# Attention in a decoder kernel: the denominators of 128 queries of a group move from TensorE to ScalarE

## The chip, the cores and the metric

The kernel runs on one core of one Trainium2 chip. The metric is the device time of one execution in microseconds (us), from the first to the last instruction and the little that lies around them; the median of several runs is quoted. Every number of one execution comes from its profile.

## What is computed

A decoder layer over 4 sequences of 512 tokens with 512 channels: attention and layer norm, then a layer in which each token goes to one of four experts, then a layer with eight routed experts and a shared one. The change lies in the attention, whose core is this:

```
qkv = x @ w_attn + b_attn
q, k, v = split(qkv)                       # 16 heads of 32 channels
att = einsum('bhqd,bhkd->bhqk', q, k) / sqrt(32)
att = where(causal, att, -inf)
att = softmax(att, axis=-1)
y = einsum('bhqk,bhkd->bhqd', att, v)
x = layernorm(x + (y @ w_proj + b_proj))
```

A softmax needs for each query and head the maximum of its scores and, as the denominator, the sum of their exponentials.

## The kernel before, in words

The attention works on **groups** of 4 heads (128 channels), 4 groups per sequence, 16 groups in all (g = 0 to 15). A sequence is cut into 4 tiles of 128 tokens. One list of steps, written out by `attention_steps`, sets the order on every engine; each engine walks the same list and does its own part of each entry. The entries that matter:

- **Q, K**: a product of 512x512 results made in three parts of four matmuls each (high times high, low times high, high times low). ScalarE writes the rounded half `ch_hi` (L624), VectorE the remainder `ch_lo` (L771). Then both are copied within SBUF to the stacked operands `qS` and `kS`, 24 transfers of 64 KB for one group: SyncE issues 20 of them (L362), ScalarE the other four, `kS` from `ch_hi` (L629), right behind K's L624. Q of the next group waits on ScalarE (L623) until all 24 have landed, since it overwrites `ch_hi`.
- **P1** (g, 0 to 9), "first scores": queries on partitions. TensorE writes one 512-column bank of `psS` (L548), VectorE adds the mask and takes the maximum (L787) into `rowmax`. `psS` has two banks, so unit n waits for the maximum of unit n-2 (L545). Units 0 to 3 hold the last 128 queries (tile 3) of one head against all 512 keys, as one block; units 4 to 7 hold a block of 384 and one of 128; units 8 and 9 two of 256.
- **M**: the maxima are transposed into four rows (L556) and ScalarE writes them, negated, as four more rows of `qS` (L647).
- **P2** (g, 0 to 9), "second scores": keys on partitions, maxima already subtracted. TensorE writes a bank of `psE` (L569), ScalarE takes the exponential into `p_f` (L657), GpSimd clears what lies above the diagonal (L424). `psE` has two banks, so unit n waits for the exponential of unit n-2 (L566).
- **PV** (g, j), in the order j = 0, 1, 3, 2: TensorE multiplies the exponentials with the values into `psO` and with ones into `psN`, which gives the denominators (L587), over (4-j)*128 query columns.
- **NORM** and **YH**: VectorE turns and inverts the denominators and scales `psO` in three parts (L794 to L804); ScalarE and GpSimd split the result (L664, L429).
- PR is the projection with `w_proj`, V the product for the values, XT and CW are transposes of inputs and of weights of the next layer, ZB adds a bias (L438, GpSimd), LN1 and LN2 are the layer norm.

**Step s** (0 to 15) overlaps three groups: Q and K of group s+2, P1 of group s+1, P2 of group s, PV of group s-1. It begins with a **head**: six product parts of Q and K, with the first three P1 units and M between them. Then PV with P1 and P2 between, then pairs of P1 and P2. Where nothing else is to be filled in, the last three P2 units (7, 8, 9) are left over and stand in the next head, one behind each part of Q. I call such steps **short**: s = 2, 3, 6, 7, 10, 11 (and step 1 is close to them). Steps 4, 8, 12 are filled with V and steps 5, 9, 13 with PR, twelve product parts each: the **long** steps. Steps 14 and 15 have no Q and K left.

Before step 0 stand Q and K of groups 0 and 1 and P1 of group 0. There ScalarE issues all 12 transfers of each K itself (L636, L640).

## Time and profile before

| | us |
|---|---|
| median of 3 runs | 1248.32 |
| lowest, highest | 1247.42, 1250.17 |
| the profiled execution | 1241.62 |
| its span, first to last instruction | 1239.9 |
| TensorE busy in the span | 1177.1 (95%) |
| VectorE, ScalarE, GpSimd busy | 683.6, 452.9, 280.7 |

The attention fills about the first 410 us of the span. Busy time of TensorE is modelled for matmuls that overlap one another, so a busy TensorE may still have been slowed by what feeds it. The trace has a view in order of time for each engine, with the wait before an instruction and what ended it in square brackets; a view by stretches; a view by groups of instructions; and the chain, which follows the work that ended last back in time.

### The profile page before, as it was taken

How to read it: one execution, taken by the hardware profiler on the slowest of the kernel's cores; microseconds unless marked ns; L12 is line 12 of the kernel's file. 1: busy time of each engine (PE TensorE's matmuls, PEld its weight loads, DVE VectorE, ACT ScalarE, POOL GpSimd, SP SyncE). 2: the span in 40 equal slices, each digit the busy share in tenths (PEclk: the TensorE clock that was granted, in tenths of full speed). 3: DMA queues.
4: the chain of work that ended last, by engine and by line, in shares of the span. 5: the costliest groups of instructions: out<-in, count | busy, mean ns of one | idle time of the engine just before them, and what ended most of it. 6: DMA issues, size and time to landing. Idle time of an engine off the chain costs nothing.

```text
span 1239.9 us, 20255 instructions
## 1 busy us (share of the span) xinstructions
PE 1177.1 (95%) x6404; PEld 930.3 (75%) x6404; DVE 683.6 (55%) x1485; ACT 452.9 (37%) x699; POOL 280.7 (23%) x405
## 2 busy tenths in 40 slices
PE   7789999999998789998999999999999998999995
PEld 6556676676675478886677888999999997778884
DVE  5575666656656547765467434434335433766744
ACT  3245434434436223322333334334434433323331
POOL 3012314414415301223122430000000001452302
PEclk8989999999999989999999999999999999999998
DMA  7347673423433233333166673344444523555530
GB/s 249 79 117 246 201 265 105 135 68 86 137 85 123 90 111 95 112 117 119 31 98 138 236 272 104 108 150 156 145 148 150 161 86 100 189 187 165 160 118 34
DMA packets 128814, 169.76 MB, mean 137 GB/s; under 512 B 18112, under 2 KB 71360, under 8 KB 128704
## 3 DMA queue, kind: packets, MB, share of 16 engines
q1 hardware_dynamic: 110368, 128.77, 34.7%
q0 software_dynamic: 10336, 32.53, 7.3%
q10 hardware_dynamic: 8000, 7.10, 2.4%
q8 instruction: 56, 0.92, 0.3%
q14 instruction: 54, 0.44, 0.1%
HBM read 95.98 MB, written 47.19 MB: 115 GB/s over the span
## 4 chain that ended last, share of the span: by engine, by line
PE 79%; DVE 7%; DMA 6%; ACTq 2%; ACT 2%; issue 2%; POOL 2%; SPq 1%; POOLq 0%; DVEq 0%
PE bank L852 28%; PE bank L913 15%; PE psT L482 12%; PE psS L548 3%; DMA shared_raw<-in_L_ffn_Sd_dram 3%; PE psO L587 3%; PE bank L1533 3%; PE bank L1534 3%; PE bank L1535 3%; PE psE L569 2%; PE psN L587 2%; PE bank L1555 1%; DVE psS L787 1%; PE bank L1578 1%; SPq L362 1%
## 5 line engine op out<-in xcount | busy, mean ns | idle before, releaser
L913 PE MATMUL bank<-store,shared_held 128*128 128x512 f32 x792 | 188.0, 393 | 3.6 <-issue 2.9
L913 PEld LDWEIGHTS bank<-store,shared_held 128*128 128x128 f32 x792 | 149.0, 189 | 38.5 <-DVE shared_held L1852 4.3
L482 PE MATMUL psT<-store 128*128 128x512 f32 x576 | 157.6, 409 | 4.3 <-DVE store L701 2.7
L657 ACT ACTIVATE acc<-psE 128x512 f32<-128x512 f32 x160 | 92.8, 598 | 133.0 <-PE psE L569 89.3
L787 DVE CUSTOM_DVE_ANT_0 psS<-psS,attn_mask 128x512 f32<-128x512 f32 (+3 forms) x256 | 120.0, 514 | 35.5 <-PE psS L548 35.2
L482 PEld LDWEIGHTS psT<-store 128*128 128x128 f32 x576 | 106.2, 196 | 24.0 <-issue 3.0
L1447 POOL DMA_INDIRECT routed_rows_io<-sorted_y,routed_pos x32 | 37.1, 1159 | 376.6 <-DMA sorted_y<-routed_rows_io 313.0
L852 PE MATMUL bank<-shared_held,routed_h_hi 128*128 x624 | 115.9, 328 | 0.3 <-DVE routed_h_lo L1893 0.3
L424 POOL TENSOR_SCALAR_AFFINE_SELECT acc<-acc 128x256 f32<-128x256 f32 (+1 forms) x160 | 56.9, 362 | 258.4 <-ACT acc L657 258.0
L852 PEld LDWEIGHTS bank<-shared_held,routed_h_hi 128*128 128x128 f32 x624 | 100.3, 188 | 0.7 <-issue 0.5
L852 PE MATMUL bank<-store 128*128 x351 | 91.5, 405 | 0.0
L548 PE MATMUL psS<-attn_kS,attn_qS 96*128 96x512 f32 (+3 forms) x256 | 73.9, 352 | 8.8 <-DVE attn_rowmax L787 4.4
L548 PEld LDWEIGHTS psS<-attn_kS,attn_qS 96*128 96x128 f32 x256 | 44.8, 196 | 48.2 <-DVE attn_rowmax L787 20.7
L569 PE MATMUL psE<-attn_qS,attn_kS 100*128 100x512 f32 (+3 forms) x256 | 69.9, 338 | 4.9 <-ACT acc L657 4.2
L852 PEld LDWEIGHTS bank<-store 128*128 128x128 f32 x351 | 63.6, 190 | 12.2
L1654 ACT ACTIVATE routed_h_f<-bank 128x512 f32<-128x512 f32 x44 | 26.3, 597 | 123.5 <-PE bank L913 123.5
L1533 PE MATMUL bank<-shared_held,routed_h_hi 128*128 128x512 f32 x176 | 69.8, 397 | 0.1
L1534 PE MATMUL bank<-shared_held,routed_h_hi 128*128 128x512 f32 x176 | 69.5, 395 | 0.0
L1535 PE MATMUL bank<-shared_held,routed_h_lo 128*128 128x512 f32 x176 | 69.2, 393 | 0.0
L913 PE MATMUL bank<-shared_held 128*128 128x512 f32 x264 | 65.0, 400 | 0.8 <-DVE shared_held L1852 0.7
L1852 DVE TENSOR_TENSOR shared_held<-shared_raw,shared_held 128x1024 fp32r<-128x1024 f32 x42 | 51.3, 1221 | 24.4 <-ACT shared_held L1641 24.2
L852 PE MATMUL bank<-shared_held,routed_h_lo 128*128 x312 | 62.7, 323 | 0.0
(273 smaller groups left out, 1995.7 us busy)
## 6 DMA issues: line engine op xcount, KB each, us to landing
sorted_x<-attn_zero SPq DMA_DIRECT2D x19, 768.0 KB, 6.3
shared_raw<-in_L_ffn_Sg_dram SPq DMA_DIRECT2D x44, 256.0 KB, 3.1
shared_raw<-in_L_ffn_Su_dram SPq DMA_DIRECT2D x44, 256.0 KB, 3.6
shared_raw<-in_L_ffn_Sd_dram SPq DMA_DIRECT2D x44, 256.0 KB, 4.8
routed_rows_io<-sorted_x SPq DMA_DIRECT2D x39, 256.0 KB, 2.9
sorted_y<-routed_rows_io SPq DMA_DIRECT2D x39, 256.0 KB, 2.1
attn_qS<-attn_ch_hi SPq DMA_DIRECT2D x128, 64.0 KB
routed_gu_raw<-in_L_ffn_Wg_dram SPq DMA_DIRECT2D x8, 704.0 KB, 4.5
```

The costliest lines, as they stand in the source:

```text
L424: pool.affine_select(out=at, in_=at, compare_op=ALU.is_ge, fill=drop, base=0, pattern=[[0, at.shape[1]], [1, P]], channel_multiplier=-1).t ...
L482: last = pe.matmul(out, lhs[a](k), rhs[c](k), start=(s[-1] == 0 and k == 0), stop=(s[-1] == 2 and k == KC - 1))
L548: last = pe.matmul(psS[:, n % 2, c0:c0 + (t + 1) * P], q[0:AUX, i, t * P:(t + 1) * P], k[0:AUX, i, 0:(t + 1) * P], start=True, stop=True)
L569: last = pe.matmul(psE[:, n % 2, c0:c0 + (QT - j) * P], k[0:AUX + 4, i, j * P:(j + 1) * P], q[0:AUX + 4, i, j * P:T], start=True, stop=True)
L587: last = pe.matmul(to[i * D:(i + 1) * D, j * P:T], values(i), p_f[:, u, c0:c0 + (QT - j) * P], start=(j == 0), stop=(j == 2), tile_positio ...
L657: act.activation(p_f[:, u, :], psE[:, n % 2, :], ACT.Exp, scale=SCALE).then_inc(exp_done, 1)
L787: last = dve.tensor_tensor_reduce(scores, scores, mask[:, (3 - t) * P:T], 1.0, BELOW_ALL, ALU.add, ALU.max, rowmax[:, g % 2, t, i:i + 1])
L852: last = pe.matmul(out, lhs[a](k), rhs[c](k), start=(n == 0), stop=(n == 3 * chunks - 1))
L913: last = pe.matmul(out, w[:, slot, at + k * P:at + (k + 1) * P], x_part(k), start=(g == 0 and k == 0), stop=(g == 2 and k == KC - 1))
L1533: pe.matmul(s_y[i], h[0], w[0], start=(c == 0), stop=False)
L1534: pe.matmul(s_y[i], h[0], w[1], start=False, stop=False)
L1535: last = pe.matmul(s_y[i], h[1], w[0], start=False, stop=(c == CH - 1))
```

## The change

Three things change in the attention, and some semaphores are merged (the constants and one-hot rows now count on one semaphore, the same instructions in the same order).

1. The denominators of tile 3, the last 128 queries, are no longer made by TensorE. ScalarE takes the exponential of the first scores in `psS` in place, with the maximum as bias, and totals each row (64 instructions, four in each group). So that both exponentials use the same maximum, VectorE rounds it (`rounded`) and scales it (`shift`), two instructions of one column behind each of those units. GpSimd spreads the totals over 128 columns, and TensorE transposes them into the last 128 columns of `psN`. The matmuls with ones shrink by 128 columns, and those of j = 3 go.
2. The P1 units come in another order of blocks, so that the four totalled ones stand at positions 3, 5, 7 and 9. The unit two behind waits for the total, no longer for the maximum.
3. ScalarE's four key transfers for group s+2 move from K in the head to behind the exponential of P2 unit 5.

```diff
+    BLOCKS = (8, 9, 4, 0, 5, 1, 6, 2, 7, 3)
     def s_segments(u):
+        u = BLOCKS[u]
...
@@ GpSimd
+                elif kind == "M":
+                    g = s[1]
+                    pool.wait_ge(total_done, 4 * (g + 1))
+                    if g >= 2:
+                        pool.wait_ge(pv_done, QT * (g - 2) + 1)
+                    pool.tensor_copy(spread_3[:, g % 2, :].rearrange("p (i d) -> p i d", d=D),
+                                     total_3[:, g % 2, :].unsqueeze(2).broadcast_to([P, 4, D])).then_inc(spread_done, 1)
...
@@ TensorE, P1
                     if n >= 2:
-                        pe.wait_ge(max_done, n - 1)
+                        of, was = divmod(n - 2, UNITS)
+                        if summed_block(was) is not None:
+                            pe.wait_ge(total_done, 4 * of + summed_block(was) + 1)
+                        else:
+                            pe.wait_ge(max_done, n - 1)
...
@@ TensorE, PV
-                    for to, values in ((psO, lambda i: v_f[...]), (psN, lambda i: ones[:])):
-                        for i in range(4):
+                    if j == 0:
+                        pe.wait_ge(spread_done, g + 1)
+                        pe.transpose(psN[:, T - P:T], spread_3[:, g % 2, :], ident[:])
+                    for to, values, upto in ((psO, lambda i: v_f[...], T),
+                                             (psN, lambda i: ones[:], T - P)):
+                        for i in range(4 if j * P < upto else 0):
...
@@ ScalarE
+            def totals(upto):
+                for n in range(summed[0], upto):
+                    g, u = divmod(n, 4)
+                    scores = psS[:, (g * UNITS + BLOCKS.index(u)) % 2, :]
+                    act.wait_ge(shift_done, 2 * n + 2)
...
+                    act.activation(scores, scores, ACT.Exp, bias=shift[:, g % 2, u:u + 1], scale=SCALE,
+                                   accum_out=total_3[:, g % 2, u:u + 1]).then_inc(total_done, 1)
+                summed[0] = max(summed[0], upto)
...
@@ ScalarE, Q and K
-                    if qk == 1 and g >= 2:
-                        act.wait_ge(hi_done, hi_order[s[:2]] + 1)
-                        for i in range(4):
-                            act.dma_start(kS[g % 3][2 * D:3 * D, i, :].bitcast(F32), ...
...
+                elif kind == "P1":
+                    g, u = s[1:]
+                    if g == 0:
+                        totals(seen[0])
+                    if summed_block(u) is not None:
+                        seen[0] = 4 * g + summed_block(u) + 1
                 elif kind == "M":
+                    totals(seen[0])
...
@@ ScalarE, P2
+                    totals(ripe[0])
+                    ripe[0] = seen[0]
                     act.wait_ge(e_full, n + 1)
...
                     act.activation(p_f[:, u, :], psE[:, n % 2, :], ACT.Exp, scale=SCALE).then_inc(exp_done, 1)
+                    if u == 5 and g + 2 < NG:
+                        g += 2
+                        act.wait_ge(hi_done, hi_order["K", g] + 1)
+                        for i in range(4):
+                            act.dma_start(kS[g % 3][2 * D:3 * D, i, :].bitcast(F32), ...
...
@@ VectorE, P1
+                    u = summed_block(u)
+                    if u is not None:
+                        dve.wait_ge(max_done, n + 1)
+                        dve.tensor_copy(rounded[:, g % 2, u:u + 1], rowmax[:, g % 2, QT - 1, u:u + 1]).then_inc(shift_done, 1)
+                        dve.wait_ge(shift_done, 8 * g + 2 * u + 1)
+                        dve.tensor_scalar(shift[:, g % 2, u:u + 1], rounded[:, g % 2, u:u + 1].bitcast(F32), -SCALE, None,
+                                          ALU.mult).then_inc(shift_done, 1)
```

Where it moves instructions shows in the order on the engines. First ScalarE in a short step, from K's rounded half to the end of the next Q; `acc<-psE` is the exponential of P2, `attn_qS<-psT` belongs to M, `attn_yT_hi` to YH. Before:

```order
L647 ACTIVATE attn_qS<-psT 4x2048
L624 ACTIVATE attn_ch_hi<-psT,attn_bqk 128x512
L629 DMA attn_kS<-attn_ch_hi 32x512 x4
L657 ACTIVATE acc<-psE 128x512 x7
L664 CAST attn_yT_hi<-acc 128x512
L657 ACTIVATE acc<-psE 128x512 x2
L624 ACTIVATE attn_ch_hi<-psT,attn_bqk 128x512
```

Now, in the same place, with line numbers of the changed kernel (L629 is a total, L701 the exponential, L706 the key transfers), from the second exponential on:

```order
L629 ACTIVATE psS,attn_total<-psS,attn_shift 128x512
L701 ACTIVATE acc<-psE 128x512 x2
L629 ACTIVATE psS,attn_total<-psS,attn_shift 128x512
L701 ACTIVATE acc<-psE 128x512 x2
L629 ACTIVATE psS,attn_total<-psS,attn_shift 128x512
L701 ACTIVATE acc<-psE 128x512
L706 DMA attn_kS<-attn_ch_hi 32x512 x4
L701 ACTIVATE acc<-psE 128x512
L714 CAST attn_yT_hi<-acc 128x512
L629 ACTIVATE psS,attn_total<-psS,attn_shift 128x512
L701 ACTIVATE acc<-psE 128x512 x2
L664 ACTIVATE attn_ch_hi<-psT,attn_bqk 128x512
```

The transfers stood ahead of the exponential of unit 0 and now stand between those of units 5 and 6; a total stands ahead of those of units 1, 3, 5 and 7, the last behind YH.

Second, ScalarE before step 0, from Q of group 1 to Q of group 2. Before:

```order
L624 ACTIVATE attn_ch_hi<-psT,attn_bqk 128x512 x2
L636 DMA attn_kS<-attn_ch_hi 32x512 x8
L640 DMA attn_kS<-attn_ch_lo 32x512 x4
L624 ACTIVATE attn_ch_hi<-psT,attn_bqk 128x512
L647 ACTIVATE attn_qS<-psT 4x2048
```

Now (L671 and L675 are the transfers of K of group 1):

```order
L664 ACTIVATE attn_ch_hi<-psT,attn_bqk 128x512
L629 ACTIVATE psS,attn_total<-psS,attn_shift 128x512 x2
L664 ACTIVATE attn_ch_hi<-psT,attn_bqk 128x512
L671 DMA attn_kS<-attn_ch_hi 32x512 x8
L675 DMA attn_kS<-attn_ch_lo 32x512 x4
L629 ACTIVATE psS,attn_total<-psS,attn_shift 128x512
L664 ACTIVATE attn_ch_hi<-psT,attn_bqk 128x512
L629 ACTIVATE psS,attn_total<-psS,attn_shift 128x512
```

Two totals of group 0 stand ahead of the twelve transfers; the third, for which P1 unit 9 of group 0 waits, behind them.

Third, TensorE in the PV part of a step. Before:

```order
L587 MATMUL psO<-acc 32x512 x4
L587 MATMUL psN<-acc,attn_ones 32x512 x4
L548 MATMUL psS<-attn_kS,attn_qS 128x512
L569 MATMUL psE<-attn_qS,attn_kS 128x512
L587 MATMUL psO<-acc 32x384 x4
L587 MATMUL psN<-acc,attn_ones 32x384 x4
```

Now (L609 is the transpose of the totals, L614 PV, L569 P1, L592 P2):

```order
L609 MATMUL psN<-ident,attn_spread 128x128
L614 MATMUL psO<-acc 32x512 x4
L614 MATMUL psN<-acc,attn_ones 32x384 x4
L569 MATMUL psS<-attn_kS,attn_qS 128x512
L592 MATMUL psE<-attn_qS,attn_kS 128x512
L614 MATMUL psO<-acc 32x384 x4
L614 MATMUL psN<-acc,attn_ones 32x256 x4
```

One transpose came in and every matmul with ones lost 128 columns; P1 and P2 stand where they stood.

## Rows read from the trace of the kernel before

**Rows 1.** Busy time by stretch: stretch, its length, then each engine, granted clock, DMA

```profile
200.00:300.00 100.00, 98.31 (x654) 67.01 (x645) 63.03 (x198) 42.76 (x66) 33.43 (x63) 1.00 0.37 101
```

**Rows 2.** The chain through step 11: start, us on the chain, what

```profile
306.04 0.60 PE psT L556 x4
...
307.79 0.99 PE psO L587 x8
308.79 0.86 PE psN L587 x8
...
311.09 0.65 PE psN L587 x8
...
312.81 0.22 PE psN L587 x8
...
314.32 0.43 PE psN L587 x8
...
325.51 0.99 PE psO L587 x8
```

**Rows 3.** ScalarE in order of time, step 11 and the next head: start, us, instruction [wait]

```profile
309.28 2.67 ACTq L629 DMA_DIRECT2D attn_kS<-attn_ch_hi  x4
...
316.94 0.60 ACT L657 ACTIVATE acc<-psE 128x512 f32<-128x512 f32 x1 [0.28 <-PE psE L569]
...
317.69 0.60 ACT L657 ACTIVATE acc<-psE 128x512 f32<-128x512 f32 x1 [0.15 <-PE psE L569]
...
319.80 0.62 ACT L664 CAST attn_yT_hi<-acc 128x512 fp32r<-128x512 f32 x1 [1.51 <-DVE acc L804]
...
320.33 1.08 ACT L657 ACTIVATE acc<-psE 128x512 f32<-128x512 f32 x2
```

**Rows 4.** TensorE in the same stretch: P1 unit 7, P2 units 6, 8 and 9

```profile
315.33 0.41 PE L548 MATMUL psS<-attn_kS,attn_qS 96*128 96x384 f32 x2
...
317.26 0.40 PE L569 MATMUL psE<-attn_qS,attn_kS 100*128 100x384 f32 x2
...
319.67 0.41 PE L569 MATMUL psE<-attn_qS,attn_kS 100*128 100x256 f32 x2
...
320.97 0.50 PE L569 MATMUL psE<-attn_qS,attn_kS 100*128 100x256 f32 x2
```

**Rows 5.** VectorE in order of time: two small instructions in a row, and one maximum

```profile
284.08 0.17 DVE L832 BATCH_NORM_AGGREGATE attn_mv<-attn_stats 128x2 f32<-128x6 f32 x1
284.28 0.15 DVE L834 TENSOR_SCALAR attn_veps<-attn_mv 128x1 f32<-128x1 f32 x1
...
306.51 0.73 DVE L787 CUSTOM_DVE_ANT_0 psS<-psS,attn_mask 128x512 f32<-128x512 f32 x1
```

**Rows 6.** ScalarE's groups by line: count, busy us, mean ns, idle before

```profile
L624 ACT ACTIVATE attn_ch_hi<-psT,attn_bqk 128x512 fp32r<-128x512 f32 x32 | 22.0, 688 | 38.8 <-PE psT L482 26.4 <-DMA attn_kS<-attn_ch_lo 12.0
```

**Rows 7.** SyncE's last four key transfers of step 11, and P1 unit 0 behind them

```profile
316.12 2.50 SPq L362 DMA_DIRECT2D attn_kS<-attn_ch_lo  x4
...
322.19 0.19 PEld L548 LDWEIGHTS psS<-attn_kS,attn_qS 96*128 96x128 f32 x1 [0.22 <-DMA attn_kS<-attn_ch_lo]
```

**Rows 8.** ScalarE and TensorE in order of time, before and in step 0

```profile
46.76 0.50 PE L548 MATMUL psS<-attn_kS,attn_qS 96*128 96x256 f32 x2
...
50.26 2.53 ACTq L640 DMA_DIRECT2D attn_kS<-attn_ch_lo  x4
...
54.28 0.50 PE L548 MATMUL psS<-attn_kS,attn_qS 96*128 96x512 f32 x1 [2.44 <-DMA attn_kS<-attn_ch_lo]
...
59.09 2.67 ACTq L629 DMA_DIRECT2D attn_kS<-attn_ch_hi  x4
...
65.08 0.79 PE L569 MATMUL psE<-attn_qS,attn_kS 100*128 100x512 f32 x1 [2.75 <-ACT acc L657]
```

**Rows 9.** TensorE in the PV part of step 4: P2 unit 2

```profile
141.95 0.51 PE L569 MATMUL psE<-attn_qS,attn_kS 100*128 100x512 f32 x1 [0.71 <-ACT acc L657]
```

More of the change, by code:

```diff
@@ L164, in key_of, with summed_block @@
         return s[:-1] if s[0] in PARTS else s
+    BLOCKS = (8, 9, 4, 0, 5, 1, 6, 2, 7, 3)
+    def summed_block(u):
+        return BLOCKS[u] if BLOCKS[u] < 4 else None
     def s_segments(u):
+        u = BLOCKS[u]
         if u < 4:
@@ L216, in attention_phase @@
         rowmax = sb("rowmax", [P, 2, QT, 4], F32)
+        rounded = sb("rounded", [P, 2, 4], F32R)
+        shift = sb("shift", [P, 2, 4], F32)
+        total_3 = sb("total_3", [P, 2, 4], F32)
+        spread_3 = sb("spread_3", [P, 2, P], F32)
         rsum = sb("rsum", [P, T // D], F32)
@@ L280, in attention_phase @@
         max_done = sem("max_done")
+        shift_done = sem("shift_done")
+        total_done = sem("total_done")
+        spread_done = sem("spread_done")
         e_full = sem("e_full")
@@ L554, in _ @@
                     pe.wait_ge(max_done, UNITS * (g + 1))
+                    pe.wait_ge(shift_done, 8 * (g + 1))
                     for t in range(QT):
-                        last = pe.transpose(out[0:4, t * P:(t + 1) * P], rowmax[:, g % 2, t, :], ident[:])
+                        maxima = rowmax[:, g % 2, t, :] if t < QT - 1 else rounded[:, g % 2, :].bitcast(F32)
+                        last = pe.transpose(out[0:4, t * P:(t + 1) * P], maxima, ident[:])
                     give(s, last)
@@ L583, in _ @@
                                 pe.wait_ge(sh_free[bank_of["V", g // 4, i]], use_of["V", g // 4, i] + 1)
-                    for to, values in ((psO, lambda i: v_f[:, j, (g % 4) * P + i * D:(g % 4) * P + (i + 1) * D]), (psN, lambda i: ones[:])):
-                        for i in range(4):
+                    if j == 0:
+                        pe.wait_ge(spread_done, g + 1)
+                        pe.transpose(psN[:, T - P:T], spread_3[:, g % 2, :], ident[:])
+                    for to, values, upto in ((psO, lambda i: v_f[:, j, (g % 4) * P + i * D:(g % 4) * P + (i + 1) * D], T),
+                                             (psN, lambda i: ones[:], T - P)):
+                        for i in range(4 if j * P < upto else 0):
                             u, c0 = E_AT[j, i]
-                            last = pe.matmul(to[i * D:(i + 1) * D, j * P:T], values(i), p_f[:, u, c0:c0 + (QT - j) * P],
+                            last = pe.matmul(to[i * D:(i + 1) * D, j * P:upto], values(i), p_f[:, u, c0:c0 + upto - j * P],
                                              start=(j == 0), stop=(j == 2), tile_position=(0, i * D))
@@ L762, in _ @@
                     then(dve.tensor_reduce(picked1, picked, AX, ALU.add))
-                    dve.tensor_copy(place[:], picked1).then_inc(place_done, 1)
-                    dve.wait_ge(place_done, 1)
+                    then(dve.tensor_copy(place[:], picked1))
                 elif kind in ("Q", "K") and s[-1] == 2:
```

34 lines of the change are left out of this document (17 added, 17 removed).

## The prediction

> **What bounds the kernel now.** Read the view by stretches first: inside the attention TensorE is busy 98% of the time at full clock, VectorE 63, ScalarE 43 [rows 1]. That invites the sum "less work for TensorE, less time". The chain through step 11 says how far it holds: of the step's 17.7 us (325.51 less 307.79) nearly all lies on TensorE, the denominators among it with 0.86, 0.65, 0.22 and 0.43 [rows 2]. Then read the other queues for how near they are. ScalarE and TensorE in order of time show that P2 units 8 and 9 come 2.4 and 3.7 us behind unit 6, and the exponentials they wait for just in time [rows 3, 4]. SyncE's twenty transfers are as near: the last is issued by 318.62, and P1 unit 0 of the next group waits 0.22 us for its landing at 322.19 [rows 7]. So in short steps three resources are level. The long steps have twelve product parts between the P1 and P2 units, and there only TensorE counts.
>
> **What TensorE saves.** The matmuls with ones run over 512, 384, 256 and 128 columns, 1280 in all, in 0.86 + 0.65 + 0.43 + 0.22 = 2.16 us [rows 2], 1.69 us for a thousand columns. The change leaves 768: 0.86 us less. It adds one transpose of 128 columns; four in M take 0.60 [rows 2], so between 0.15 and, with a weight load that nothing hides, 0.3; 0.2 taken. Net 0.65 us a group, 10.4 for 16 groups, if nothing else moves.
>
> **What the others get.** VectorE: two small instructions behind each of 64 maxima. Two such in a row stand 0.20 us apart [rows 5]: 0.4 a unit, 26 us in all, hidden at 63% busy except where someone waits for that unit. ScalarE: 64 exponentials of 128x512 with a column as bias. An exponential without one takes 0.60 [rows 3], a pass with one 0.69 [rows 6]; the total of a row, which no row shows, may add something like nothing or another 0.14. 0.69 taken, the ends 0.60 and 0.83. 44 us in all, again hidden except on a chain. GpSimd: 16 copies of 128x128, early enough for PV a step later: nothing. The block order itself: the same columns, nothing. The merged semaphores: nothing.
>
> **The new chain.** P1 unit 9 waits for the total of unit 7: matmul 0.4, maximum 0.73 [rows 5], two small ones 0.4, total 0.69, hand-offs 0.1: 2.3 us. Before it was 0.4 + 0.73. And the exponential of unit 5 stands behind that total on ScalarE.
>
> **A short step, walked through in the clock of step 11.** Before, P1 unit 7 starts at 315.33, P2 unit 6 at 317.26, unit 8 at 319.67, unit 9 at 320.97 [rows 4]. After:
> - The four PV parts ahead save 0.65; the total of unit 5 takes some 0.15 back. P1 unit 7 at 314.8.
> - Its total is ready 2.3 later, 317.1, so P1 unit 9 starts at 317.15 and P2 unit 6 at 317.45. The saving is already gone, 0.2 late.
> - ScalarE: the exponential of unit 5 until 317.7, then the four key transfers. In the head they take 2.67 [rows 3] and delay the first exponential, but PV lies there and TensorE doesn't wait. Here they end at 320.4, and the exponential of unit 6, which before followed at 317.69 [rows 3], ends at 321.0. P2 unit 8 at 321.1: 1.4 late.
> - Queued behind: YH 0.62 [rows 3], the total of unit 9 0.69, the exponential of unit 7 0.60, ends 322.95. P2 unit 9 at 323.0: 2.0 late.
> - Two waits go: the 0.22 of P1 unit 0 [rows 7] and about as much ahead of M. Left: 1.6 at the end of the step; over six short steps, two of which have more idle time there, **1.5 each, +9.0**.
>
> The figure that weighs most is 0.67 us for one issue on ScalarE. The Trainium skill ("DMA: Bandwidth & Descriptors", Anatomy of one DMA — SWDGE (gpsimd) path) gives about 50 ns for a sequencer's dispatch, of which the data's travel is no part. By it four issues hold ScalarE 0.2 us, a short step loses some 0.3 instead of 1.5, and the kernel would come out near 1250.5. The trace has 2.67 for four on this very queue, and the trace decides.
>
> **The start.** Totals of group 0 stand in ScalarE's order at the P1 steps. That of unit 7, for which P1 unit 9 waits, comes behind K of group 1 and its twelve transfers, the last issued by 52.79 [rows 8]. So unit 9 starts at 53.5 and not at 46.76. TensorE had 2.44 us of waiting ahead of P1 unit 0 of group 1 [rows 8], which cover a part: +4.3. In step 0 the four transfers (2.67 at 59.09) leave the way of the first exponential, for which P2 unit 2 waited 2.75 at 65.08 [rows 8]: -2.7. But no PV lies between the P1 units there, and units 5, 7 and 9 each wait for a total: 2.3 in place of two maxima, 1.5: three times 0.8, less what is hidden, +1.9. Together **+3.5** (bounds +1 and +6: the first if the twelve issues turn out hidden by the wait on landing, the second if nothing is hidden).
>
> **The rest.** Step 1, nearly a short one, with two transposes between that cover the wait for the total: +1.2. Six long steps: at least four filled slots lie between the exponentials of unit 5 and unit 8, some 5 us, which hide transfers and totals: 0.65 gained each, -3.9. In step 4 the wait of 0.71 behind slow transfers [rows 9] goes: -0.7. Step 14 is paced by VectorE (maxima, layer norm, splits), where the small instructions come on top: 4 x 0.4 less 0.65, +1.0. In step 15 GpSimd's wait for its input hides all: 0. The last PV: -0.65.
>
> **Sum**: 9.0 + 1.2 + 3.5 - 3.9 - 0.7 + 1.0 - 0.65 = +9.4 us. On the profiled execution's 1241.6 that is 1251.0; the median of the runs is 6.7 above it, so 1248.3 + 9.4 = **1257.7 us**.
>
> **The rivals.**
> - **TensorE's saving comes through.** If the exponential of unit 6 is not late, since the issues are shorter there or the step has slack that rows 4 don't show, each group keeps its 0.65: 10.4, and 0.7 and 2.7 for the transfers that leave the head, less 4.3 at the start: -9.5, **1238.8**. For it: 98% busy [rows 1], the chain on TensorE [rows 2]. Against it: the order of unit 6 behind the transfers. The Trainium skill ("Perfetto Trace Analysis", Identifying the Most-Contended Engine) tells to optimize the engine with the highest occupancy first; here that is TensorE, and by it this rival would win.
> - **The two cancel.** Short steps lose 0.3 and not 1.5, the start and the rest as above: 9.4 - 7.2 = +2.2, about 1250; a cheaper start brings it to 1247. It decides by how long ScalarE is held between the exponentials of units 5 and 6: below about 1.4 us P2 unit 8 no longer waits.
> - **The key transfers land too late.** Issued by 320.4 and landing 3.6 us behind the issue, as SyncE's do (318.62 to 322.19, rows 7), they come at 324.0, just when P1 unit 0, now at 323.8, wants them; and Q's rounded half waits for all 24. It bites from a landing of over 3.6 us on. With 2 us more in each short step: +12 on top, **1269**. For it: zero-filling transfers are in flight in steps 1 to 5 and an input load in steps 7 and 11.
>
> **How the numbers follow.** The forecast, a loss of 4 to 16 us, gets 0.58; the saving coming through 0.20; cancelling 0.10; late transfers 0.12. The range: the forecast's case runs from 1252 to 1264 by the ends of the total's price (0.6 to 0.83, twice in a short step: 2 to 3 us) and of the start. It reaches down into the first rival, to 1240, and up to most of the last, 1268; outside lie about 0.1 below and 0.05 above. About 0.2%, 2.5 us, is what a measurement of this kernel can tell from no change. Faster by more: 0.21, the first rival and a sliver of the second. Within: 0.10. Slower by more: 0.69.
>
> **What would show it.** In the profile after: TensorE busy some 7 to 10 us less, the span longer; P2 units 8 and 9 of short steps waiting on the exponential for 1 us and more; the transfers in one piece of 2.6 us on ScalarE between two exponentials; short steps of 19.2 us and long ones shorter by 0.65; P1 unit 9 of group 0 near 53.5. It would be wrong if P2 unit 8 doesn't wait, if the totals take well over 0.83, or if P1 unit 0 waits for transfers.

## The result and the profile after

The changed kernel takes **1276.7 us** (median of four runs, 1272.9 to 1282.9) against 1247.9 for the kernel before, run beside it: 1.025 times as long, with a 95% interval of 1.0222 to 1.0279. The forecast was 1257.7 in a range of 1240 to 1268. The sign was right; the loss is 29 us and not 9, and the time lies above the range. The profiled executions stand 35.5 us apart (spans 1275.4 and 1239.9), and that is what the traces have to explain; some 6 us of it are the pick, since the profiled execution of before (1241.6) lies that far below the median of its runs and that of after (1277.1) does not.

A table by step tells where. A step reaches from the first psO product of one group, TensorE's `128x512`, to that of the next; "start" is all ahead of the first, "rest" all behind the sixteenth. The steps of before are read in the same way. us:

```
            start   1     2     3     4     5     6     7     8     9    10    11    12    13    14    15   rest
before       79.8  20.5  17.6  17.6  28.7  30.7  18.0  18.3  27.8  30.8  18.0  17.7  27.8  22.1  16.8  11.8  836.0
after        89.2  26.2  20.7  20.1  27.9  31.8  18.9  21.2  27.8  31.2  18.9  21.2  27.8  22.0  17.8  14.6  838.1
difference   +9.4  +5.7  +3.1  +2.5  -0.8  +1.1  +0.9  +3.0   0.0  +0.4  +0.9  +3.5  -0.1   0.0  +0.9  +2.8   +2.1
forecast     +3.5  +1.2  +1.5  +1.5  -1.3  -0.7  +1.5  +1.5  -0.7  -0.7  +1.5  +1.5  -0.7  -0.7  +1.0    0    -0.7
```

Each column is one execution. How far single steps wander shows in e4_order_only and e16_key2_late below, whose times cannot be told from before: there one step is 1.4 us longer (step 3 of e4) and "rest" is 4.7 and 5.5 us longer. So the 2.1 us in "rest" need no cause, and a difference of one step counts where it comes back in others.

The short steps 6 and 10 grew by less than forecast, 7 and 11 by twice as much, and the two kinds have the same work. The view by stretches, of steps 10 and 11 of after and then of before, shows what differs: the column before the last two is the granted clock of TensorE.

```profile
315.00:333.91 18.91, 16.82 (x119) 10.95 (x118) 15.21 (x50) 12.08 (x23) 7.03 (x12) 1.00 0.41 111
333.91:355.10 21.19, 19.49 (x118) 13.37 (x118) 12.62 (x46) 12.29 (x23) 12.70 (x22) 0.84 0.49 152
```

```profile
289.75:307.72 17.97, 17.62 (x125) 10.90 (x125) 13.78 (x42) 9.22 (x15) 6.80 (x11) 1.00 0.39 103
307.72:325.44 17.72, 17.58 (x125) 10.81 (x125) 11.13 (x38) 9.33 (x15) 10.42 (x17) 1.00 0.61 191
```

So step 11 lost 0.9 us to waiting, as step 10 did, and the 2.3 us beyond that go with the clock: 0.84 is an average of 1.0 (2.4 GHz) and 0.5 (1.2 GHz). TensorE in order of time shows both. These rows answer to [rows 4]; a bracket is the wait ahead of the instruction and who ended it.

```profile
338.76 0.50 PE L569 MATMUL psS<-attn_kS,attn_qS 96*128 96x512 f32 x1 [0.18 <-ACT psS L629]
...
341.30 0.50 PE L569 MATMUL psS<-attn_kS,attn_qS 96*128 96x512 f32 x1 [0.29 <-ACT psS L629]
...
343.84 0.80 PE L569 MATMUL psS<-attn_kS,attn_qS 96*128 96x512 f32 x1 [1.22 <-ACT psS L629]
...
344.86 2.02 PE L499 MATMUL psT<-store 128*128 128x512 f32 x4
...
347.10 2.02 PE L499 MATMUL psT<-store 128*128 128x512 f32 x4
...
352.12 1.09 PE L499 MATMUL psT<-store 128*128 128x512 f32 x4
```

P1 units 5, 7 and 9 wait 0.18, 0.29 and 1.22 us for the totals of units 3, 5 and 7. Four products of 512 columns take 1.09 us at 352.12 and 2.02 right behind the wait of 1.22. The wait of 1.22 stands in each of the six short steps; the granted clock is 0.92, 0.84 and 0.84 in steps 2, 7 and 11 and stays at 1.00 in 3, 6 and 10. So the wait alone does not decide where the clock falls.

Over the whole span the mean granted clock is 0.979 before and 0.965 after. That is some 52 and 89 us at the half clock, and since the products take no more than twice as long there, the clock can account for at most about 18 of the 35.5 us (an estimate from these two means and spans).

The total itself is two instructions on ScalarE, and the pair takes 0.79 us on the chain:

```profile
L629 ACT ACTIVATE psS<-psS,attn_shift x64: 653/662/696, 42.5 to 421.3; 128x512 f32<-128x512 f32 x64
L629 ACT ACTIVATION_READ_ACCUMULATOR psS<-psS,attn_shift x64: 192/193/225, 43.0 to 421.9; 128x1 f32 x64
```

TensorE's waits by cause, summed over the kernel (us, times, longest). In the kernel before the first line has no counterpart:

```profile
PE psS L569 <- ACT psS L629: 28.1, 36, 6.7
PE psS L569 <- DVE attn_rowmax L836: 4.3, 4, 2.0
...
PE psS L569 <- DMA attn_kS<-attn_ch_hi: 3.8, 3, 2.1
```

The longest is in the start, [rows 8] after the change. ScalarE, then TensorE:

```profile
46.80 5.10 ACTq L671 DMA_DIRECT2D attn_kS<-attn_ch_hi  x8
51.94 2.52 ACTq L675 DMA_DIRECT2D attn_kS<-attn_ch_lo  x4
54.51 0.66 ACT L629 ACTIVATE psS<-psS,attn_shift 128x512 f32<-128x512 f32 x1 [7.74 <-issue]
```

```profile
55.34 0.80 PE L569 MATMUL psS<-attn_kS,attn_qS 96*128 96x512 f32 x1 [6.67 <-ACT psS L629]
55.93 6.72 PE L499 MATMUL psT<-store 128*128 128x512 f32 x20
62.49 0.40 PE L569 MATMUL psS<-attn_kS,attn_qS 96*128 96x256 f32 x2
```

The twenty products behind that wait take 6.72 us; before they took 4.74:

```profile
47.10 4.74 PE L482 MATMUL psT<-store 128*128 128x512 f32 x20
```

And the chain through steps 1 to 3 has key transfers that it did not have, while SyncE issues zero-fills. TensorE waits 2.07, 0.90 and 0.85 us for keys at the end of these steps:

```profile
103.22 7.21 DMA attn_kS<-attn_ch_hi
...
126.47 6.22 DMA attn_kS<-attn_ch_hi
...
147.15 5.62 DMA attn_kS<-attn_ch_hi
```

```profile
99.44 4.36 SPq L342 DMA_DIRECT2D sorted_x<-attn_zero  x4
```

### The profile page after: what moved, and what is told of

Its sections match the earlier page's. It is cut to its first block, busy times and chain, and to the rows that moved or that the text cites. A ratio compares the mean times of both kernels' runs of the same rounds, so it can differ in the third digit from the quotient of the medians.

```text
span 1275.4 us, 20331 instructions
## 1 busy us (share of the span) xinstructions
PE 1182.2 (93%) x6292; PEld 941.7 (74%) x6292; DVE 705.3 (55%) x1613; ACT 498.2 (39%) x827; POOL 284.6 (22%) x421
## 4 chain that ended last, share of the span: by engine, by line
PE 73%; DVE 9%; DMA 6%; ACT 6%; issue 2%; ACTq 2%; POOL 2%; SPq 0%; POOLq 0%; DVEq 0%
PE bank L908 27%; PE bank L969 16%; PE psT L499 12%; DVE psS L836 3%; PE bank L1589 3%; PE bank L1590 3%; PE bank L1591 3%; PE psS L569 3%; ACT psS L629 2%; DMA shared_raw<-in_L_ffn_Sd_dram 2%; DMA attn_kS<-attn_ch_hi 1%; ACT attn_qS L689 1%; PE bank L1611 1%; PE psE L592 1%; PE bank L1634 1%
## 5 line engine op out<-in xcount | busy, mean ns | idle before, releaser
L969 PEld LDWEIGHTS bank<-store,shared_held 128*128 128x128 f32 x792 | 147.9, 188 | 39.9 <-DVE shared_held L1908 6.0
L499 PE MATMUL psT<-store 128*128 128x512 f32 x576 | 167.8, 429 | 3.8 <-DVE store L751 2.2
L836 DVE CUSTOM_DVE_ANT_0 psS<-psS,attn_mask 128x256 f32<-128x256 f32 (+3 forms) x256 | 120.8, 510 | 29.7 <-PE psS L569 28.3
L701 ACT ACTIVATE acc<-psE 128x512 f32<-128x512 f32 x160 | 94.2, 597 | 94.1 <-PE psE L592 83.5
L499 PEld LDWEIGHTS psT<-store 128*128 128x128 f32 x576 | 112.5, 208 | 24.6 <-issue 2.6
L569 PE MATMUL psS<-attn_kS,attn_qS 96*128 96x256 f32 (+3 forms) x256 | 77.1, 365 | 37.4 <-ACT psS L629 28.1
L569 PEld LDWEIGHTS psS<-attn_kS,attn_qS 96*128 96x128 f32 x256 | 46.7, 197 | 74.0 <-ACT psS L629 38.8
L592 PE MATMUL psE<-attn_qS,attn_kS 100*128 100x512 f32 (+3 forms) x256 | 71.3, 345 | 4.9 <-ACT acc L701 2.7
L908 PEld LDWEIGHTS bank<-store 128*128 128x128 f32 x351 | 63.6, 190 | 12.2
L820 DVE SCALAR_TENSOR_TENSOR attn_ch_lo<-psT,attn_bqk,attn_ch_hi 128x512 fp32r<-128x512 f32 x32 | 24.0, 749 | 76.1 <-ACT attn_ch_hi L664 76.1
```

The source lines that it names most:

```text
L499: last = pe.matmul(out, lhs[a](k), rhs[c](k), start=(s[-1] == 0 and k == 0), stop=(s[-1] == 2 and k == KC - 1))
L569: last = pe.matmul(psS[:, n % 2, c0:c0 + (t + 1) * P], q[0:AUX, i, t * P:(t + 1) * P], k[0:AUX, i, 0:(t + 1) * P], start=True, stop=True)
L592: last = pe.matmul(psE[:, n % 2, c0:c0 + (QT - j) * P], k[0:AUX + 4, i, j * P:(j + 1) * P], q[0:AUX + 4, i, j * P:T], start=True, stop=True)
L701: act.activation(p_f[:, u, :], psE[:, n % 2, :], ACT.Exp, scale=SCALE).then_inc(exp_done, 1)
L836: last = dve.tensor_tensor_reduce(scores, scores, mask[:, (3 - t) * P:T], 1.0, BELOW_ALL, ALU.add, ALU.max, rowmax[:, g % 2, t, i:i + 1])
L908: last = pe.matmul(out, lhs[a](k), rhs[c](k), start=(n == 0), stop=(n == 3 * chunks - 1))
```

## The experiments

The theories that the expectations name. **A**: late keys land behind zero-fills, and totals hold P1. **B**, the prediction's own: the late issues stand between exponentials and hold P2. **C**, formed after the first runs: P1 waits for a chain of maximum, two copies and total. Its rival, named beside it in e6, e8 and e9: the work that ScalarE and VectorE got costs in itself, wherever it stands. **D**: a wait as in C brings the half clock. Each ratio is to the kernel before on the same chip, with its 95% interval; the kernel after has 1.0250.

### The parts of the change

**e1_keys_early.** After, with one part undone:

```
+                    if qk == 1 and g >= 2:
+                        ...four key transfers behind K, as before
-                    if u == 5 and g + 2 < NG:
-                        ...
```

> The kernel after, with the four key transfers of a group put back where the kernel before issues them, behind the upper half of the keys (K), not behind the exponential of unit 5. Theory A (transfers queued late land behind the zero-fills of steps 1 to 3, and the totals hold P1): only the key share of steps 1 to 3 comes back. These steps grew by 5.7, 3.1 and 2.5 us; part of that is the wait of P1(g+1, 0) for its keys, 7.21 and 6.22 us from issue to landing on the chain of waits. So 1265 to 1269 us, with steps 7, 11 and 15 still some 3 us longer than before. Theory B (the step of my prediction: the issues stand between the exponentials of units 5 and 6 and hold P2 unit 8): steps 7 and 11 shrink by the 1.5 us each that were forecast, all short steps together by 9, and steps 1 to 3 by no more than those; 1266 us as well, but with the gain spread evenly over steps 2, 3, 6, 7, 10, 11. The step table tells them apart, not the time.

Measured 1284.7 us, 1.0297 (1.0273 to 1.0321): neither. Undoing this part makes the kernel slower by some 6 us, as totals then stand behind the issues in every step. TensorE's waits for totals rose from 28.1 to 39.9 us:

```profile
PE psS L569 <- ACT psS L629: 39.9, 39, 6.7
```

**e2_keys_only.** Before, with the same move alone.

> The kernel before, with nothing changed but the place of the four key transfers: behind the exponential of unit 5. No totals, no new order of units. Theory A: steps 1 to 3 grow by some 2 us each (P1(g+1, 0) waits for keys that land behind zero-fills), other steps by under 0.3: 1250 to 1254 us. Theory B: the six short steps by 1.5 each, 1257 us. If the late issue is free without the totals, 1248.

Measured 1253.6 us, 1.0073 (1.0051 to 1.0095): +2.7 in step 1, +0.5 and +0.4 in steps 2 and 3, +2.9 in step 5, +0.8, +0.7, +0.1 and +0.7 in steps 6, 7, 10 and 11, and 1.8 less at the start. The sum is A's and not B's 9, the pattern is neither's: A had 2 us in each of steps 1 to 3 and under 0.3 elsewhere, and step 5 stays unexplained. The issues between exponentials cost a short step at most 0.8 and not 1.5. The same move costs the kernel before 0.7% and saves the kernel after about 0.5%.

**e3_no_totals.** After, without the ScalarE instruction:

```
-                    act.activation(scores, scores, ACT.Exp, bias=shift[...], scale=SCALE,
-                                   accum_out=total_3[...]).then_inc(total_done, 1)
...
-                        if summed_block(was) is not None:
-                            pe.wait_ge(total_done, 4 * of + summed_block(was) + 1)
-                        else:
-                            pe.wait_ge(max_done, n - 1)
+                        pe.wait_ge(max_done, n - 1)
```

> The kernel after, without the 64 totals on ScalarE: their 0.79 us each are gone, P1 waits for the maxima alone, and the denominators of each group's last 128 queries are left out (a constant 1 is spread in their place). The copies rounded and shift on VectorE, the order of the units, the shorter psN products and the late key transfers stay. Theory A: the start comes back by some 7 us of its 9.4, steps 7, 11 and 15 by 3 each, the half clock behind the waits of P1 units 5, 7 and 9 goes, and the shorter products now save their 0.65 a group; what is left is the wait for late keys in steps 1 to 3: 1245 to 1253 us. Theory B (issues between exponentials are the cost): 1262 to 1268, since these stay.

Measured 1246.1 us, 0.9998 (0.9982 to 1.0014). **The 64 totals, with what waits for them, cost 2.5%, 31 us, the whole loss.** Without them the start is 1.5 us shorter than before. B is out as the cause of the loss. The parts do not add up one by one: late keys cost the kernel before 0.7% and this one nothing.

**e4_order_only.** Before, with `BLOCKS` in the order of units for P1.

> The kernel before with the units of scores for the maxima in the order of the kernel after (8, 9, 4, 0, 5, 1, 6, 2, 7, 3) and nothing else. Both theories: no cost of its own, within 0.3% of before, 1246 to 1251 us. If the new order puts the longest chain of VectorE (two-part units with masks) at the end of P1, M would be late and each step longer by up to 0.7 us, 1258.

Measured 1246.7 us, 0.9998 (0.9974 to 1.0023): no effect.

### The 31 us of the totals

**e6_short_totals.** `scores = psS[:, ..., 0:64]` in place of the whole bank: only the totals' duration changes.

> The kernel after, with each total run over the first 64 of its 512 columns: the instructions, their order and their waits stay, only their time falls, from 0.79 to some 0.35 us by the fixed part; the denominators of the last 128 queries are then sums over 64 keys. Theory C, the wait of P1 for a chain of maximum, two copies and total: unit 9 in short steps waits 1.22 and would wait 0.8, with less half clock behind: 10 to 16 us come back, 1261 to 1267. If instead ScalarE's load of work as such (51 us a hundred against 43) is what costs, the time it holds falls by 28 us and the same comes out, but in the long steps as well, 1 us each. If it is the mere order (waits at fixed places behind other work) it stays above 1270.

Measured 1262.7 us, 1.0139 (1.0102 to 1.0176): 14 us come back by the duration alone. That is what C expected, and its rival as well. The pair of instructions now takes 0.29 and 0.19, and TensorE's waits for totals fell from 28.1 to 16.9 us:

```profile
L629 ACT ACTIVATE psS<-psS,attn_shift x64: 279/288/324, 40.6 to 403.4; 128x64 f32<-128x64 f32 x64
...
PE psS L569 <- ACT psS L629: 16.9, 16, 6.5
```

Step 1 took 5.6 us less and step 7 2.8 less than in the kernel after; steps 8, 12 and 13 0.6 less each, so that the long steps had been losing theirs to the totals too. Step 11 took 1.5 more: P1 unit 0 waits 2.95 us for the late keys there, in a step with an input load in flight.

**e5_start_fix.** `if s == ("K", 1, 2): totals(3)` ahead of the twelve transfers.

> The kernel after, with one thing moved on ScalarE: the total of unit 7 of group 0 comes ahead of the twelve key transfers of group 1, not behind them. Theory C (what the four runs so far leave: totals cost 31 us, of which the start and step 0 hold 11): P1(0, 9) no longer waits 6.67 us for the issues; of the 11 us some 4 to 6 come back, since the waits behind single totals and the half clock stay in part: 1270 to 1273. If the transfers, now later, are missed by P1(1, 0), whose wait was 2.44 us before, no more than 1 us comes back: 1276.

Measured 1275.3 us, 1.0236 (1.0201 to 1.0272), not to be told from the kernel after: the miss that the second sentence named. P1(0, 9) waits 0.88 in place of 6.67, but the transfers are issued until 56.9 and P1(1, 0) waits for them:

```profile
50.11 0.50 PE L569 MATMUL psS<-attn_kS,attn_qS 96*128 96x512 f32 x1 [0.88 <-ACT psS L629]
...
58.37 0.80 PE L569 MATMUL psS<-attn_kS,attn_qS 96*128 96x256 f32 x2 [3.20 <-DMA attn_kS<-attn_ch_lo]
```

**e13_no_totals_start.** After, where `totals` skips the groups 0 and 1.

> The kernel after without the totals of groups 0 and 1 (their denominators of the last 128 queries are left out); those of groups 2 to 15 stay. By the profiles the time to the first PV and step 1 hold 10.9 and 3.5 of the 31 us that totals cost, but of step 1's only the half clock belongs to the start: 1276.7 less 11 to 14 is 1263 to 1266. If the start's loss is taken up later by a wait that is there anyway, 1270 and above.

Measured 1270.6 us; the kernel before took 1249.1 on this chip, so the ratio counts: 1.0151 (1.0115 to 1.0186), 12 us below the kernel after. That is within the 11 to 14 expected, with some 4 us to either side: two groups of sixteen carry about two fifths of the cost. In the profile the first PV is 9.1 us earlier, at 80.1.

**e7_warm.** After, with ten transposes ahead of the wait of P1 unit 9 in six steps:

```
+                    if u == 9 and g in (3, 4, 7, 8, 11, 12):
+                        pe.wait_ge(exp_done, (g - 1) * UNITS + 5)
+                        for _ in range(10):
+                            pe.transpose(psE[:, 0, 0:P], ident[:], ident[:])
```

> The kernel after, with ten transposes of 128x128 ahead of the wait of P1 unit 9 in the steps 2, 3, 6, 7, 10 and 11, into a bank that the next unit of P2 overwrites: TensorE is busy in the 1.22 us in which it waited for the total of unit 7. Theory D, that such a wait brings the half clock (steps 3, 7 and 11 have 3.4, 6.8 and 6.8 us at half clock that the kernel before has not, the fall each time within a us of this wait): these stretches go, 6 to 9 us come back less 0.2 for each set that runs past the wait: 1267 to 1272. If the clock falls for another reason, it stays at 1277 or comes out above by 1.

Measured 1277.0 us, 1.0239 (1.0200 to 1.0278): no gain, so D's 6 to 9 us did not come. In the profile steps 7 and 11 run at full clock and fall from 21.2 to 18.9 us, the length of steps 6 and 10; step 3, which had the transposes as well, has the half clock (0.86):

```profile
241.68:260.59 18.91, 17.91 (x128) 12.03 (x127) 12.63 (x46) 12.06 (x23) 11.62 (x18) 1.00 0.58 172
338.49:357.40 18.91, 17.95 (x128) 12.03 (x127) 12.63 (x46) 12.06 (x23) 11.55 (x18) 1.00 0.58 175
```

```profile
137.23:161.19 23.96, 21.27 (x129) 13.81 (x128) 12.63 (x46) 12.38 (x23) 9.93 (x16) 0.86 0.65 206
```

The work that fills the wait costs nothing (P1 unit 9 starts no later, 9.93 us into step 11 in both), and a stretch at half clock goes with 2.3 us more in a step. That the wait brings it is not shown. What was gained in two steps was lost in the start and in step 3, and the mean clock of the execution is 0.964 against 0.965. Nor is the full clock in steps 7 and 11 shown to be the transposes' doing: e5, e12 and e13 keep all six waits, and of the steps 6, 7, 10 and 11 the clock falls there in 7 and 10, in 7, 10 and 11, and in 7 and 10.

**e8_placed.** After, with the summed units elsewhere:

```
-    BLOCKS = (8, 9, 4, 0, 5, 1, 6, 2, 7, 3)
+    BLOCKS = (8, 4, 0, 1, 2, 5, 6, 7, 3, 9)
...
-                    totals(ripe[0])
-                    ripe[0] = seen[0]
+                    if u < 4 or u == 8:
+                        totals((ripe if u < 4 else seen)[0])
```

> The kernel after with its 64 totals whole, but at other places: the four summed units of a group are units 2, 3, 4 and 8 (order of blocks 8, 4, 0, 1, 2, 5, 6, 7, 3, 9), and ScalarE takes the totals of units 2 to 4 ahead of the exponentials of units 0 to 2 and that of unit 8 ahead of the exponential of unit 8. Between unit n and unit n + 2 there TensorE has 4.0, 3.2 and 2.8 us of other work (step 11 after), more than the chain of 2.5, and unit 8 is waited for in the next step alone. Theory C: the waits of P1 for totals go and most of the 31 us come back: 1247 to 1253, the key transfers' 7 us still in it. If what costs is the work that ScalarE and VectorE got in itself, wherever it stands: 1265 to 1277.

Measured 1269.9 us, 1.0168 (1.0113 to 1.0224): about a third of the way. C's 1247 to 1253 is missed, and the time lies in its rival's range. The trace says where C holds and what stood in its way. Steps 6 and 10 are 18.2 and 18.4 us, within 0.4 of before, with all the added work in them; P1 still waits 0.51 us for one total in each. So C is right for a step that has nothing else, and the work in itself costs it little. TensorE's waits for totals fell to 16.9 us. But its waits for keys rose from 3.8 to 12.2. They stand in steps 1 to 3, where P1 unit 0 of the next group now comes sooner and the keys don't, and in steps 7 and 11, with 3.21 us in step 11:

```profile
PE psS L569 <- ACT psS L629: 16.9, 18, 4.4
PE psS L569 <- DMA attn_kS<-attn_ch_hi: 7.5, 3, 2.8
PE psS L569 <- DMA attn_kS<-attn_ch_lo: 4.7, 3, 3.2
```

**e9_placed2.** The same, with key transfers behind K in steps 1 to 3, one total earlier in the start, and that of unit 2 ahead of the key transfers in steps 0 to 3.

> The kernel of the run before with the totals of units 2, 3, 4 and 8 (1269.9 us, four runs from 1262 to 1277), and three more moves: in the start the total of unit 8 of group 0 stands ahead of Q of group 2, where P1(1, 0) waited 3.90 us for it; in steps 0 to 3 the total of unit 2 stands ahead of the key transfers; in steps 1 to 3, where zero-fills run, the key transfers stand behind K again. Theory C with late landing as a second cause: P1's waits for keys of 2.77, 2.31 and 2.40 us and the two of 3.90 and 4.41 in the start go, with part of the half clock behind them: 12 to 18 us less, 1252 to 1258. If what is left of the loss lies in the work added to ScalarE, it stays above 1263.

Measured 1269.5 us, 1.0219 (1.0177 to 1.0261): missed, and again where the rival would have it, but the trace has waits for it. The start fell by 3.9 us against e8, and the waits for keys in steps 1 to 3 went; in their place the total of unit 3 stands behind the four issues, and P1 unit 5 waits for it. ScalarE and TensorE in step 2:

```profile
109.93 1.25 ACTq L673 DMA_DIRECT2D attn_kS<-attn_ch_hi  x2
...
111.21 1.25 ACTq L673 DMA_DIRECT2D attn_kS<-attn_ch_hi  x2
...
113.06 0.66 ACT L629 ACTIVATE psS<-psS,attn_shift 128x512 f32<-128x512 f32 x1
```

```profile
113.88 0.80 PE L569 MATMUL psS<-attn_kS,attn_qS 96*128 96x384 f32 x2 [2.05 <-ACT psS L629]
```

### The late keys and the zero-fills

**e10_keys_clears.** e2_keys_only, and in SyncE's queue:

```
-                    if g >= 3 and qk == 1:
+                    if g in (6, 7, 10, 11, 14) and qk == 1:
                         for _ in range(min(4, len(pieces))):
                             clear()
```

> The kernel before with late key transfers (1253.6 us alone) and with the zero-filling transfers of sorted_x issued at K of groups 6, 7, 10, 11 and 14, in long steps, and not at K of groups 3 to 7. Theory: late keys cost 7 us since they land behind zero-fills in steps 1 to 3; without these they cost nothing, step 0 keeps the 1.8 that it gains, and step 1's +2.7 goes: 1244 to 1248 us. If they cost 7 us by their place on ScalarE, it stays at 1252 to 1255.

Measured 1248.1 us, 1.0022 (1.0007 to 1.0036) against 1.0073 with the zero-fills in place. Step 1 lost its +2.7 and its wait of 0.82 for keys. **Of the 0.7% that late keys cost the kernel before, 0.5% goes with the zero-fills**, and 0.2% remains. What moving the zero-fills does to the kernel before by itself was not run.

**e12_clears_after.** The kernel after with the same edit.

> The kernel after with the zero-fills moved to the long steps (K of groups 6, 7, 10, 11, 14). P1(g+1, 0) waits 2.07, 0.90 and 0.85 us for keys in steps 1 to 3, and the chain of waits has 7.21 and 6.22 us from issue to landing there. By these waits 4 us come back, with less half clock behind them up to 8: 1268 to 1273. If the zero-fills have no part, 1276.

Measured 1267.2 us, 1.0179 (1.0158 to 1.0200), by the ratio 9 us below the kernel after and a little more than expected. Step 1 fell from 26.2 to 21.1, steps 2 and 3 from 20.7 and 20.1 to 19.3 and 18.9. TensorE no longer waits for keys in steps 1 to 15, and its waits for totals stay as they were (28.4 us).

### What could be had at most

**e11_no_totals_early.** e3_no_totals with the key transfers as before.

> The kernel without the ScalarE totals (1246.1 us; the denominators of each group's last 128 queries are left out), with the key transfers back behind K as in the kernel before. The most that this change could bring if its totals were free. By adding up: 1246.1 less the 7.3 that late keys cost alone is 1238.8; if the shorter products bring nothing with early keys, 1246.

Measured 1247.7 us, 1.0023 (1.0006 to 1.0041): no gain.

**e15_no_totals_clears.** e3_no_totals with the zero-fills moved.

> The kernel without ScalarE totals (1246.1 us; the denominators of each group's last 128 queries are left out), key transfers late, zero-fills in long steps: the most that the change can bring where neither totals nor zero-fills are in the way. Late keys with moved zero-fills alone gave 1248.1, 5.4 less than with them in place; shorter products 7.5 less in one pair of runs (1253.6 and 1246.1) and nothing in the other (1246.7 and 1247.7). So 1241 if they add up, 1247 if the products' saving was made of waits for late keys.

Measured 1249.1 us, 1.0006 (0.9982 to 1.0029), no gain again. Three kernels whose totals cost nothing, because they aren't there, are no faster than the kernel before. In e15 the long steps 8, 12 and 13 are 0.5 to 0.8 shorter and step 4 is 1.7 shorter; steps 2, 3, 6, 7, 10 and 11 stand between -0.3 and +0.7, and steps 9, 14 and 15 are 2.2, 1.3 and 1.8 longer. In step 14 VectorE sets the pace: it is busy 16.0 of 16.8 us there before the change.

**e14_placed3.** All repairs in one: e8's places, e12's zero-fills, and in the start the totals of units 8 and 2 ahead of Q and of the last transfers of K.

> The kernel after with its totals whole and the three repairs that showed an effect: totals of units 2, 3, 4 and 8, late key transfers with zero-fills in long steps, and in the start the total of unit 8 ahead of Q of group 2 and that of group 1's unit 2 ahead of the last four transfers of K. From 1267.2 (zero-fills moved): 5.6 at the start, 0.6 in each of six short steps, 1.5 where half clock follows: 1255 to 1259. It is then still slower than before; at 1249 or less the change could be had.

Measured 1262.3 us against the 1255 to 1259 expected; by the ratio, 1.0089 (1.0059 to 1.0119), 11 us above before and 20 below after. Against e15_no_totals_clears above, on the same chip and with the keys and zero-fills in the same places but no totals, that is 10 us. The start is 3.9 us longer than there, steps 6, 8, 10, 12 and 13 are 0.7 to 0.8 longer, and in each of these five P1 waits 0.51 us for a total: even well placed, one total a step is waited for. Besides, P1 unit 0 waits 1.01 and 1.37 us for keys in steps 7 and 11. The half clock is nearly gone from the attention (0.99), which after the change has 0.97:

```profile
83.40:418.30 334.90, 308.09 (x2031) 210.55 (x2030) 221.66 (x730) 183.40 (x338) 112.57 (x215) 0.99 0.48 144
```

```profile
89.16:437.32 348.16, 316.72 (x2031) 219.34 (x2030) 222.57 (x730) 186.60 (x338) 112.77 (x215) 0.97 0.46 138
```

**e16_key2_late.** Before, with `if qk == 1 and g >= 3` at K and the late transfers for group 2 alone.

> The kernel before with the four transfers of group 2's keys alone behind the exponential of unit 5 of step 0. Every run with late keys had its first PV 1.5 to 1.9 us earlier, since the exponentials of step 0 no longer stand behind them: 1244 to 1246, 0.15% less. Step 1 may give it back, where P1(2, 0) waits for these keys: then 1247.

Measured 1248.7 us against 1249.1, 0.9986 (0.9964 to 1.0008). The profile has the first PV 2.1 us earlier, the time can't be told from no change. No kernel here is shown to beat the kernel before.

## Why the prediction was wrong

The direction followed from the idea that the ScalarE chain eats TensorE's saving, and that held. By its steps:

- **What bounds the kernel.** "In short steps three resources are level" held: without totals (e3, e11, e15) steps 6, 7, 10 and 11 are at most 0.3 shorter. In e11, with the keys early, TensorE waits in them 0.18 for a maximum, 0.37 for an exponential, and 0.35 for VectorE's remainder or 0.6 to 0.9 for SyncE's keys. The Trainium skill ("Perfetto Trace Analysis", Identifying the Most-Contended Engine) would have the engine with the highest occupancy optimized first. Three kernels relieved TensorE of the columns and won nothing.
- **What TensorE saves.** 0.65 a group was right where TensorE alone counts: without totals the steps 8, 9, 12 and 13 are 0.9, 0.6, 0.8 and 0.8 shorter. Wrong was that a long step hides the totals: step 8 after has P1 waits of 0.20 and 0.29 for them and ends even, steps 5 and 9 have one of 0.76. The sum has -3.9 and -0.7 for the long steps; they measured +0.6 together.
- **The price of a total.** 0.69 taken, 0.60 to 0.83 as ends; it is 0.79, in two instructions. The term is small but stands in a chain that was cut too tight: 2.3 us, in truth 2.54 (338.76, 341.30, 343.84 in the rows above).
- **Four transfers between two exponentials hold P2.** The failed step: it had P2 unit 8 of a short step 1.4 us late and unit 9 2.0, and most of the 9.0 us for the short steps come from it. ScalarE in step 11:

```profile
343.01 0.66 ACT L629 ACTIVATE psS<-psS,attn_shift 128x512 f32<-128x512 f32 x1 [0.33 <-DVE attn_shift L844]
343.01 1.17 ACTq L706 DMA_DIRECT2D attn_kS<-attn_ch_hi  x2
...
343.69 0.59 ACT L701 ACTIVATE acc<-psE 128x512 f32<-128x512 f32 x1
344.21 1.26 ACTq L706 DMA_DIRECT2D attn_kS<-attn_ch_hi  x2
345.52 0.60 ACT L701 ACTIVATE acc<-psE 128x512 f32<-128x512 f32 x1 [1.25 <-PE psE L592]
```

  The issues do take 0.61 each. The 50 ns that the Trainium skill gives ("DMA: Bandwidth & Descriptors", Anatomy of one DMA — SWDGE (gpsimd) path) are not what ScalarE pays here; that section describes a transfer issued from GpSimd. But the issues begin with the total that stands ahead of them in the queue and run beside it and the exponential of unit 5. The prediction laid them end to end behind that exponential. Here they end at 345.47, when P2 unit 6 has barely come (344.43, 0.63). In step 10, at full clock, ScalarE and then TensorE:

```profile
325.30 1.26 ACTq L706 DMA_DIRECT2D attn_kS<-attn_ch_hi  x2
326.61 0.60 ACT L701 ACTIVATE acc<-psE 128x512 f32<-128x512 f32 x1 [1.24 <-PE psE L592]
```

```profile
325.27 0.40 PE L592 MATMUL psE<-attn_qS,attn_kS 100*128 100x384 f32 x2
...
329.42 0.51 PE L592 MATMUL psE<-attn_qS,attn_kS 100*128 100x256 f32 x2 [0.39 <-ACT acc L701]
```

  Unit 6 is there at 325.67 and its exponential starts when the issues are over (326.56), 0.9 late. But P2 unit 8 waits in no short step, which the prediction named as a sign of being wrong, and unit 9 waits 0.37 to 0.39 in steps 3, 6 and 10. e2 gives the issues 0.1 to 0.8 a short step.
- **Short steps, 1.5 each.** In steps 6 and 10 it is 0.9, by another cause: P1's three waits for totals, 1.69 in all, less the columns saved. The walk put unit 9 0.2 us late for its total and laid the rest on the issues; that wait and the two before it are the whole 0.9. The other four grew by 2.5 to 3.5.
- **The missing term: the clock.** The prediction asks nowhere what TensorE's clock does if TensorE begins to wait, though the row of before has it at 1.00 for 100 us [rows 1]. It goes with 2.3 us in each of steps 7 and 11 and 2 us in the twenty products at 55.93, and by the mean clocks it is at most about 18 us in all. TensorE's busy time, forecast to fall by 7 to 10 us, rose by 5.1 (1177.1 to 1182.2). e14, which has the highest mean clock of the kernels with whole totals (0.975), has also the smallest loss. How much of the 31 us is the clock's isn't settled beyond that bound, since e7 moved the half clock and didn't remove it.
- **The start, +3.5.** The wait was found and its place was right, the size wasn't: P1(0, 9) starts at 55.34 and not 53.5, since totals ahead of K put the issues off by 1.7 us; twenty products then run at half clock. P1(1, 0) is 8.2 us late and not 4.3. e13 prices the first two groups at 12 us.
- **The rivals.** "Key transfers land too late", at 0.12, named the zero-fills of steps 1 to 5 as what speaks for it. This is a part of the truth: e12 gives back 9 us by moving them. It was priced at 2 us in each of six short steps. It acts in two of them, steps 2 and 3, where P1 unit 0 waits 0.90 and 0.85 us for keys, and most in step 1, with 2.07, which got +1.2 in the sum. The input load that the rival named for steps 7 and 11 shows in other kernels (2.95 us in step 11 of e6) and not in this one. The late landing and the waits for totals add up in one kernel; the prediction treated them as cases of which one would come true, and that cut the range at 1268.
- **Step 14** was right (+0.9 for +1.0). **Step 15** was not: +2.8 for 0. P2 unit 0 waits 1.60 us there for M's result, which stands behind a total, two exponentials and two casts on ScalarE; but two of the three kernels without totals have +1.6 and +1.8 as well, so that isn't all, and the rest stays open.

## What to carry to other kernels

When work moves from the busiest engine to an idle one, look at which buffer the new reader holds and how soon its writer comes back. Here 64 totals of 0.79 us on an engine that was 43% busy cost 31 us. A bank was to be had again after 2.54 us, and at unit 9 its writer came after 1.32 (2.54 less the wait). Shorter totals gave 14 us back, moved zero-fills 9, other places some 10, and all repairs together (without the shorter totals) 20. Price first what the shorter work brings with the new reader left out; here that is nothing, and it takes one run to see. And where waiting begins on a TensorE that had run at full clock throughout, allow in the range for stretches at the half clock.

## What the runs showed of the hardware

- An activation that sums its row is followed by an instruction of its own, 0.19 us; 0.66 and that together take 0.79 on the chain. With 64 in place of 512 columns it is 0.29 and 0.19.
- A DMA issue on ScalarE begins while activations ahead of it in the queue still run (343.01, both). What stands behind the issues waits for all of them.
- Small transfers issued behind zero-fills of 768 KB landed 5.6 to 7.2 us after their issue; the median of ScalarE's 72 of that kind is 2.2 us. With the zero-fills moved (e12) TensorE waited for none of them.
- Four products of 512 columns: 1.09 us at full clock, 2.02 at half. With the same six waits of 1.22 us, the half clock fell in other steps from one kernel to the next, and filling the waits with ten transposes left the mean clock of the execution where it was (0.964 and 0.965).
